# Attention over pixels, three small edits: order of the inverted sums, GpSimd's second weights, products of zeros

## The reference

```python
xf = x.reshape(B, Cc, N)                               # (4, 256, 1024)
q = jnp.einsum('oc,bcn->bon', Wq, xf) + bq[None, :, None]
k = jnp.einsum('oc,bcn->bon', Wk, xf) + bk[None, :, None]
v = jnp.einsum('oc,bcn->bon', Wv, xf) + bv[None, :, None]
scores = jnp.einsum('bqi,bqj->bij', q, k)
attn = jax.nn.softmax(scores, axis=-1)
out = jnp.einsum('bcj,bij->bci', v, attn)
return out.reshape(B, Cc, W, H) + x
```

## Time and profile before

| | |
|---|---|
| median of 3 runs | 165.82 us (165.29 to 167.39) |
| profiled execution | 165.86 us, of which the span is 164.1 us |
| TensorE's products | 157.8 us busy, 797 |
| VectorE | 134.5 us busy |
| ScalarE | 109.4 us busy |
| GpSimd | 56.6 us busy |

### The profile page before, as it was taken

How to read it: one execution, slowest core, us unless ns; L and a number is a source line. 1 busy time by engine, 2 the same in 40 slices (tenths; PEclk the granted TensorE clock), 3 DMA queues, 4 the chain that set the end, 5 groups by cost and what they waited for, 6 DMA issues and landing times.

```text
span 164.1 us, 2469 instructions
## 1 busy us (share of the span) xinstructions
PE 157.8 (96%) x797; PEld 131.9 (80%) x797; DVE 134.5 (82%) x214; ACT 109.4 (67%) x200; POOL 56.6 (34%) x66
## 2 busy tenths in 40 slices
PE   7799999999999999999999999999999999999993
PEld 5478778797688898788788898789888898888882
DVE  3599999886988989996999989895988679856851
ACT  3658998869799656746999665645896655756400
POOL 6079973344143303733343300241433300024600
PEclk9999999999999999999999999999999999999999
DMA  4586670452011130165310330053220330003003
GB/s 143 196 300 169 232 232 28 96 135 78 4 48 39 58 128 0 38 145 192 128 48 1 100 128 2 16 147 82 83 97 1 96 128 0 0 1 132 0 0 128
DMA packets 7636, 14.67 MB, mean 89 GB/s; under 512 B 1488, under 2 KB 1928, under 8 KB 7624
## 3 DMA queue, kind: packets, MB, share of 16 engines
q1 hardware_dynamic: 6872, 13.59, 25.7%
q0 software_dynamic: 608, 0.80, 2.3%
q10 hardware_dynamic: 144, 0.13, 0.2%
HBM read 4.79 MB, written 4.20 MB: 55 GB/s over the span
## 4 chain that ended last, share of the span: by engine, by line
PE 83%; POOL 7%; DMA 2%; ACT 2%; DVE 2%; issue 1%; SPq 0%; POOLq 0%; DVEq 0%; ACTq 0%
PE acc L970 30%; PE acc L976 16%; PE slot L823 10%; PE st L957 8%; PE slot L883 7%; PE slot L970 5%; POOL x_lo L409 3%; DMA x_sb<-x 2%; PE slot L976 2%; POOL x_hi L407 2%; PE slot L835 2%; PE slot L840 2%; DVE scaled L733 1%; ACT k_a L530 1%; POOL w_lo L401 1%
## 5 line engine op out<-in xcount | busy, mean ns | idle before, releaser
L401 POOL TENSOR_TENSOR w_lo<-w_full,w_hi 128x512 fp32r<-128x512 f32 x21 | 28.1, 1337 | 53.8 <-PE acc L976 34.1
L970 PE MATMUL acc<-w_hi,v_hi 128*128 128x512 f32 x112 | 44.7, 399 | 0.3 <-DVE scaled L733 0.2
L970 PE MATMUL acc<-w_hi,v_lo 128*128 128x512 f32 x112 | 44.2, 394 | 0.0
L518 ACT ACTIVATE w_full<-st 128x512 f32<-128x512 f32 x62 | 36.7, 592 | 7.2 <-PE st L957 7.1
L480 ACT ACTIVATE dump<-slot,negmax 128x1024 f32<-128x1024 f32 x29 | 32.4, 1119 | 10.4 <-DVE negmax L641 9.9
L641 DVE TENSOR_REDUCE negmax<-slot 128x1 f32<-128x1024 f32 x29 | 35.3, 1218 | 3.2 <-PE slot L883 2.8
L976 PE MATMUL acc<-w_lo,v_hi 128*128 128x512 f32 x112 | 36.5, 397 | 0.3 <-POOL w_lo L401 0.3
L707 DVE TENSOR_TENSOR w_lo<-w_full,w_hi 128x512 fp32r<-128x512 f32 x43 | 31.7, 740 | 3.3
L970 PEld LDWEIGHTS acc<-w_hi,v_hi 128*128 128x128 f32 x112 | 21.1, 189 | 6.7 <-issue 0.8
L976 PEld LDWEIGHTS acc<-w_lo,v_hi 128*128 128x128 f32 x112 | 21.0, 188 | 5.5 <-POOL w_lo L401 0.7
L970 PEld LDWEIGHTS acc<-w_hi,v_lo 128*128 128x128 f32 x112 | 21.2, 189 | 4.6
(11 more groups left out here) (103 smaller groups left out, 217.5 us busy)
## 6 DMA issues: line engine op xcount, KB each, us to landing
out<-x_sb SPq DMA_DIRECT2D x7, 512.0 KB, 2.8
x_sb<-x SPq DMA_DIRECT2D x3, 1024.0 KB, 6.1
k_b<-k_a SPq DMA_DIRECT2D x8, 192.0 KB, 2.6
q_b<-q_a SPq DMA_DIRECT2D x8, 192.0 KB, 2.7
x_sb<-x SPq DMA_DIRECT2D x2, 512.0 KB, 4.3
k_a<-qk_parts SPq DMA_DIRECT2D x12, 64.0 KB, 2.2
q_a<-qk_parts SPq DMA_DIRECT2D x12, 64.0 KB, 2.2
k_a<-qk_parts POOLq DMA_DIRECT2D x6, 64.0 KB, 2.1
```

The source lines that it names most:

```text
L401: nc.gpsimd.tensor_tensor(w_lo[:, r, :], w_full[:, r, :], w_hi[:, r, :].bitcast(fp32), ALU.subtract).then_inc(w_split_pool, 1)
L518: nc.scalar.activation(w_full[:, r, :], st_home(n), ACT.Exp).then_inc(exp_done, 1)
L970: nc.tensor.matmul(dst, v[:, b % 2, j, c * P:(c + 1) * P], w_hi[:, n % RING, part], start=(j == 0 and v is v_hi), stop=False)
```

## The change

Three edits. (1) The inverted sums are stored in the order of the pixels, t x 128 + p instead of p x 4 + t, so that the store writes 512 single numbers far apart where it wrote 128 runs of 4; the multiplications then read `inv_all` and `acc` as they lie, where they read `inv_all` at every fourth number. (2) `prepare_x1` is cut in two, and GpSimd takes `w_lo` of tile 1 between the cast and the subtraction of the last quarter of x. (3) 22 products of zeros at the start instead of 17.

```diff
@@ SyncE
             sp.wait_ge(inv_ready, 1)
-            sp.dma_start(inv_row.rearrange("(p t) -> p t", p=P), inv[:, :]).then_inc(inv_put, DMA)
+            with nc.allow_non_contiguous_dma("512 numbers, long ahead of their use"):
+                sp.dma_start(inv_row.rearrange("(t p) -> p t", p=P), inv[:, :]).then_inc(inv_put, DMA)
             sp.wait_ge(inv_put, DMA)
@@ GpSimd
-            def prepare_x1(i):
+            def cut_x1(i):
                 if i == 0:
                     pool.wait_ge(x1_in, DMA)
                 nc.gpsimd.tensor_copy(x_hi[:, 1, :, quarter(i)], x_sb[:, 1, :, quarter(i)]).then_inc(x1_cut, 1)
+
+            def split_x1(i):
                 pool.wait_ge(x1_cut, i + 1)
                 nc.gpsimd.tensor_tensor(x_lo[:, 1, :, quarter(i)], x_sb[:, 1, :, quarter(i)],
                                         x_hi[:, 1, :, quarter(i)].bitcast(fp32), ALU.subtract).then_inc(x1_split, 1)
...
             pool.wait_ge(shift_ready, 1)
-            prepare_x1(2)
+            cut_x1(2)
+            split_x1(2)
             pool.wait_ge(x1_split, 3)
-            prepare_x1(3)
+            cut_x1(3)
+            pool.wait_ge(x1_cut, 4)
+
+            for n in range(AHEAD):
+                split_w(n)
+            pool.wait_ge(w_split_pool, 1)
+            split_x1(3)
             pool.wait_ge(x1_split, 4)
-            for n in range(TILES):
+            for n in range(AHEAD, TILES):
@@ VectorE, finish
-                    nc.vector.tensor_tensor(scaled[:, c, :].rearrange("p (t q) -> p t q", t=TH),
-                                            acc[:, c, :].rearrange("p (t q) -> p t q", t=TH),
-                                            inv_all[:, :].rearrange("p (q t) -> p t q", t=TH),
+                    nc.vector.tensor_tensor(scaled[:, c, :], acc[:, c, :], inv_all[:, :],
                                             ALU.mult).then_inc(acc_read, 1)
@@ TensorE
             pe.wait_ge(idle_made, 1)
-            keep_busy(17, QUARTER)
+            keep_busy(22, QUARTER)
```

More of the change, by code:

```diff
@@ L429, in _ @@
             pool.wait_ge(q2_lo_put, 1)
-            prepare_x1(0)
+            cut_x1(0)
+            split_x1(0)
             pool.wait_ge(x1_split, 1)
-            prepare_x1(1)
+            cut_x1(1)
+            split_x1(1)
             pool.wait_ge(x1_split, 2)
             pool.wait_ge(shift_ready, 1)
-            prepare_x1(2)
+            cut_x1(2)
+            split_x1(2)
             pool.wait_ge(x1_split, 3)
-            prepare_x1(3)
+            cut_x1(3)
[4 more added lines that the diff above has]
+            split_x1(3)
             pool.wait_ge(x1_split, 4)
-            for n in range(TILES):
+            for n in range(AHEAD, TILES):
                 b, more = n // PER, n // PER + 1 < BATCH
```

## The result

The changed kernel takes 169.41 us (median of six runs, 168.45 to 172.23), the kernel before 165.91 beside it (165.29 to 167.39): a ratio of 1.019, 95% interval 1.012 to 1.026. The forecast was 165.9 us and a range up to 166.9. The profiled execution took 168.45 us, with a span of 166.7 where before had 164.1. In what follows a DMA is issued when its instruction runs, its packets are the pieces in which its data moves, and it has landed when the last of its 16 signs has reached the semaphore.

What follows compares the result with a forecast made beforehand. TensorE, its products filling 96% of the span, was taken as the bound. 0.75 - 0.66 + 0 = +0.09 us on the profiled 165.86 gave 165.95, and 165.9 for the median; 8-in-10 range 164.3 to 166.9.

Steps and rivals of the forecast that it cites:

- the price of the store in part 2: SyncE's store of inverted sums: 384 more packets cost at most 2.4 us, landing at 30.6, hidden from TensorE.
- rival 4: SyncE's queue: the store of 4-byte pieces delays copies into `k_a` and `q_a` for image 1's scores; 174 us, chance 0.05.
- point of decision: SyncE's wait on the store: once the store takes over 5.1 us, TensorE pays one for one.
- Part 1: GpSimd's `w_lo` of tile 1 first: 0.57 us won, then VectorE's cast and `w_lo` held, leaving TensorE 0.75 late.
- rival 3: Multiplications at L733 stay slow despite unbroken operands, leaving only the +0.75: 166.6 us, chance 0.08.
- Rivals 1 and 2: GpSimd's moved subtraction holds nobody, 164.6 us, chance 0.18; or holds only VectorE's cast, 165.1 us, chance 0.13.
- Part 2's gain: Multiplications at L733 with unbroken operands take 1.40 us together instead of 2.06, saving 0.66 on TensorE's path.
- Part 3: Five more products of zeros at TensorE's start end before the input is there; taken as 0 us.

Runs made afterwards that it cites:

- the order alone: Kernel before with only the store in pixel order and the unbroken multiplications: 171.45 us, ratio 1.031.
- the store beside: Kernel before, its own store kept, plus a second store of the same 512 numbers in pixel order to a tensor nobody reads: 167.44 us, ratio 1.010.
- the old order with the rest of the change: Changed kernel with the old store and strided multiplications; GpSimd's moved `w_lo` and 22 products of zeros stay: 166.75 us, ratio 1.005.
- all of it: Kernel before with sums transposed before storing, unbroken multiplications, GpSimd's x subtraction after `w_lo` of tile 4, 22 zeros, GpSimd's shift wait earlier: 164.67 us, ratio 0.989.
- the turned store: Kernel before with unbroken multiplications, inverted sums transposed by VectorE and stored as 16 runs of 128 bytes: 165.9 us, ratio 0.998.
- the moved wait: Kernel before with GpSimd's wait for VectorE's shift parts put ahead of the subtraction of x's second quarter: 165.78 us, ratio 0.999.
- the late subtraction: Kernel before with GpSimd taking `w_lo` of tiles 1 and 3 first, x's last subtraction only after VectorE's `w_lo` of tile 4: 165.98 us, ratio 0.998.

## Why the prediction was wrong

**The step that failed** is the price of the store in part 2: "At that price 384 more over 16 engines are 24 x 0.098 = 2.4 us, my upper bound ... Landed at 30.6 and read back by 34.9 ... Hidden." The term was taken from the time of packets. Those were even cheaper than said: the trace's packet records of the changed kernel show 8 to 9 ns for each, all over by 26.3, so by packets alone the store would have cost almost nothing. Its last sign came at 32.90, 6.6 us behind its last packet; in the kernel before it was 0.4 us. The delay isn't in the packets, and their mean time was no upper bound for it. So the sum, which held the store for hidden and took nothing for it, lacked 2.40 us of wait before the second half's scores and 0.47 behind it. The store took 7.9 us in the changed kernel, 8.3 alone and 8.6 with nothing beside it.

**The place was in the prediction, as rival 4, with 0.05.** Its point of decision, a store over 5.1 us, was passed, and its sign came: the first copy to `k_a` left at 33.49, later than 32.3. Its mechanism as written (the copies late, TensorE paying) is what the order alone showed, 3.87 us. Its price of 174 rested on a store cut over four engines, for which nothing speaks. And in the changed kernel the copies were nearly in time; what came late were the shift rows from GpSimd's queue, of which the prediction said nothing. It looked only at who stands behind the store in SyncE's queue, not at who shares the DMA engines with it; the store beside that nobody waits for shows that this is enough for harm. Why the rows took 5.1 us in the changed kernel is shown only in part. They were issued 0.7 us and more after the store had landed, and no packet of any transfer moved from 34.12 to 35.69; of the 3.2 us that the second of them was late, 1.9 passed before its packets ended and 1.3 behind them, while broadcast and copies moved. That broadcast and copies crowd the DMA engines can explain the second part, hardly the idle stretch. What held the packets there is open.

**Part 1 was right**, in its mechanism and size. Forecast: cast ending 24.85, `w_lo` ending 26.62, TensorE 0.75 late. Measured in the changed kernel: 24.65 and 26.35 with input 0.29 earlier, and 0.77. GpSimd's next `w_lo` began ahead of VectorE's by 0.23, as forecast, and the old order with the rest of the change took 166.75, against 166.6 in rival 3. Rivals 1 and 2 are out.

**Part 2's gain was right**: 0.64 us each instead of 1.03, where 0.70 was forecast, and 0.77 on the path for 0.66. Rival 3 is out.

**Part 3 was right** for the median: 165.73 against 165.59 beside it. Its reason, that the zeros end before the input is there, holds for the execution that it read and not for all. Where the cast of x began at 4.50 the first product started at 5.28 with 17 zeros (the store beside) and at 5.59 with 22 (all of it), 0.3 us later. Nor did 22 make the clock rise early: it rose between 4.07 and 7.05 in the profiles with 22, between 4.32 and 10.14 in those with 17.

**The rest of the miss**, 0.96 us of the median, goes with the clock: three of the six runs had a lower mean. Where it fell in them no trace shows. In the changed kernel's profile it stayed at 1.0 through the stalls of 0.44 and 2.24 us, and in that of the order alone it fell after one of 3.87. The prediction priced a late operand at its length and 0.12 us, which held for the 0.4 us stall.

**The chances.** A store of 4-byte pieces had no row of its own in the trace, and the packets priced were far larger ones. A bound taken across such a gap deserved more than 0.05 beyond it, above all since the threshold of 5.1 us lay only 1.3 above 1.4 + 2.4.

## What to carry to other kernels

- Price a small store by its landing, not by its packets, and if no such pattern is in the trace measure it behind the last output: six stores in one run gave it here. 128 to 512 single numbers side by side in DRAM took 8 to 10 us; the same 2 KB as runs of 16 bytes or as 4 rows of 512 took about 1.5. To change the order of a few numbers, turn them on chip (0.20 us on VectorE) and store runs (3.3 us for the four stores here).
- A slow DMA also holds back the completion of others that come after it, of other queues too, as the rows beside the store that nobody waited for; ask of each added transfer what else lands in its time.
- An instruction moved on GpSimd out of TensorE's way may fall onto VectorE's: the move here cost 0.77 us, and with the subtraction put behind VectorE's `w_lo` of tile 4 it won 0.43.

## What was not expected of the hardware

- 512 numbers of 4 bytes: 8.60, 4.28, 2.74, 2.25 and 1.75 us at 4, 8, 16, 32 and 64 bytes from start to start; 128 of them side by side 9.82.
- A broadcast whose data had moved by 30.1 was reported at about 36.1, when the store ahead of it was through.
- For 1.57 us, from 34.12 to 35.69, no DMA packet moved in the changed kernel, with the slow store landed and rows, broadcast and copies issued.
- GpSimd's subtraction holds even VectorE's operation on 128 x 4 numbers: 1.25 us for 0.17.
- The kernel before runs in two groups 1.5 us apart at a granted clock of 1.0 in both (one run 0.99). The four variants with 22 zeros and no slow store in them show no gap over 0.54 us (32 runs), while the turned store and the moved wait, with 17, show one of 0.95 and 0.85 and the late subtraction one of 0.62. Whether the zeros are what does it wasn't tried apart: with them alone the ten runs spread evenly over 1.6 us. The cause is open.
